# One layer with attention and routed experts on one core: normalised strips packed into two halves of 128 rows for the output projection, biases added to x by GpSimd

## The chip, the core and the metric

The kernel runs on one core of a Trainium2 chip. The core has five engines that run side by side, each with its own instruction stream: PE (TensorE, matrix products, with the weight loads PEld), DVE (VectorE), ACT (ScalarE), POOL (GpSimd) and SP (SyncE, which here only issues DMAs; ACT and POOL can issue DMAs too). They wait for one another by semaphores that the code sets by hand. The metric is the time of one execution on the device in microseconds (us); lower is better.

## What is computed

The input is x of shape 8 x 512 x 256 (8 sequences). The reference, cut:

```python
xn = layernorm(x)
kqv = xn @ W_kqv + b_kqv                      # 16 heads of 16
attn = softmax(q @ k.T / 4 + alibi(slopes), causal)
y = (attn @ v) @ W_proj + b_proj
# experts: 8, each token goes to one of them
probs = softmax(xn @ Wg); each expert takes its 512 best tokens; the rest go to their best expert
ffn = weight * gelu(xn @ W1[e]) @ W2[e]
out = x + y + ffn
```

## The kernel before

**Prologue (0 to 115 us).** Rows are normalised, turned and multiplied with W_kqv; keys and queries go to DRAM in parts (`k_parts`, `q_parts`), values stay in `vt`. At its end PE computes the part of the output that comes from the biases: the value bias goes through W_proj, since softmax weights sum to one. The result is added to row 16 of the projection weights `wp`, which has four groups g of 128 rows each, in which only rows 32j to 32j+16 are in use (head j of the group at 32j, its row of ones at 32j+16).

**The loop (115 to 529 us).** A row n of the loop is one sequence, with four groups g of four heads; G = 4n+g. A group has ten slots k; the pair (g,k) says where in a row something stands. In each slot PE computes a piece of the scores (`scores`), ACT takes the exponential of it into `pr_all` (line 735), GpSimd clears the future part of the diagonal blocks (`affine_select`, lines 605 and 608), and PE multiplies with the values one group later (`with_v`, line 1138, at slots 3 and 6). Beside that, PE and DVE already compute the row maxima of the next sequence (`max_unit`, `row_max`), from which `shift_rows` makes the shift of the exponent. ACT copies a group's product to `ysb` (`copy_y`, line 718), DVE makes the reciprocal of the sums (`invert`), and GpSimd multiplies (`normalise`, line 579). The result is a strip `yn` of 128 rows in which head j of the group stands at rows 32j to 32j+15.

**Projection.** The strips of sequence n-1 are projected in row n. PROJECT gives the slots: each tile t of 128 tokens takes four matmuls, one a group, in two pieces of two. DVE adds the result to x (`residual`, line 874, at the slots of RESIDUAL) in `xr`; SP stores the sum and loads the next x.

```python
PROJECT = {(2, 2): (0, (0, 1)), (2, 3): (0, (2, 3)), (2, 5): (1, (0, 1)), (2, 6): (1, (2, 3)),
           (2, 8): (2, (0, 1)), (2, 9): (2, (2, 3)), (3, 3): (3, (0, 1)), (3, 4): (3, (2, 3))}
RESIDUAL = {(2, 4): 0, (2, 7): 1, (3, 0): 2, (3, 5): 3}
```

**Routing.** In rows 0 to 3 DVE searches the experts' limits by bisection; in row 4 (ROUTED) it assigns tokens (`routing`), and PE counts marks in bank 7, which the projection also uses, so that the first projection of that row waits for `marks_read`. In rows 5 and 6 GpSimd scatters the tokens, four indirect DMAs a group (line 582). Also in the loop, a quarter of an expert matrix a group is loaded by SP, split by ACT and GpSimd into two f16 parts and stored. At the start of row 7 SP loads all the parts back with four DMAs of 2 MB each (lines 429, 431 and 432); they overwrite buffers of the loop (`xnp`, `vt`, `qs`).

**The tail (529 to 555 us) and the experts (555 to 675 us).** SP loads sorted rows (a DMA transpose, line 444) and token numbers (line 447), PE begins with the up products of three expert tiles, and projects the last sequence between them (`last_row`); DVE adds, SP stores the sum of x and attention, and GpSimd gathers it by token and scatters the output. The experts' loop is bound by PE.

**What sets the order.** The order on each engine is the order of its code, by slots as in the tables; SP's is the program order of its block: per group `store_quarter`, `load_quarter`, at g=3 also `shift_rows`, `store_sum`, `load_x`, and then, after a wait for the group's scores, `load_group` for two rows ahead.

## Time and profile before

| | |
|---|---|
| median of 3 runs | 688.47 us (686.81 to 691.18) |
| the profiled execution | 688.02 us, span 686.2 us |
| PE, weight loads | 561.0 us (82%), 334.7 us (49%) |
| DVE | 413.5 us (60%) |
| ACT | 331.1 us (48%) |
| POOL | 328.5 us (48%) |
| DMA queue of SP, of POOL, of ACT | 36.2%, 8.6%, 2.0% of 16 engines |
| chain that ended last | PE 40%, DVE 26%, POOL 12%, issue 10%, ACT 5%, DMA 4% |

The span is the time from the first to the last instruction in the profile; the execution's time has 1.8 us around it. A share of busy time is a mean over stages with different limits, so the stretches and the timeline of each stage are read beside it.

### The profile page before, as it was taken

What the parts mean: (1) busy time and instruction counts of PE and PEld (TensorE: products, weight loads), DVE (VectorE), ACT (ScalarE), POOL (GpSimd) and SP (SyncE); (2) the same over time, 40 slices, a digit from 0 to 9 for tenths busy, and PEclk for the clock granted to TensorE, in tenths of its full rate; (3) what the DMA queues carried; (4) which work ended last, traced back from release to release, by engine and by line L of the source; (5) the groups of instructions that cost most, each with busy time, mean ns of one, the idle gap of its engine ahead of it and who ended that gap; (6) DMA issues with size and microseconds to landing.
All of it is one profiled execution on the core that took longest, in us unless ns stands there. A gap on an engine that the chain in (4) does not pass through costs nothing.

```text
span 686.2 us, 13215 instructions
## 1 busy us (share of the span) xinstructions
PE 561.0 (82%) x4515; PEld 334.7 (49%) x4515; DVE 413.5 (60%) x819; ACT 331.1 (48%) x623; POOL 328.5 (48%) x481
## 2 busy tenths in 40 slices
PE   1878488648888989989975979998887989999992
PEld 0445254324334534535433534545333878787782
DVE  4655435959999688797798688585322333333331
ACT  3454454207665565555652456575664333333330
POOL 5647110303444354343441338787863277655552
PEclk9999799959999999999998999999999999999997
DMA  4698787591323151241421135353488445654310
GB/s 138 188 255 119 238 279 258 189 278 56 110 64 102 57 171 55 86 139 55 142 86 54 57 116 156 115 174 101 124 288 288 89 117 136 120 109 110 93 48 8
DMA packets 100671, 92.12 MB, mean 134 GB/s; under 512 B 36658, under 2 KB 89843, under 8 KB 100599
## 3 DMA queue, kind: packets, MB, share of 16 engines
q1 hardware_dynamic: 90336, 69.69, 36.2%
q0 software_dynamic: 6576, 17.91, 8.6%
q10 hardware_dynamic: 3696, 3.67, 2.0%
q8 instruction: 40, 0.66, 0.4%
q14 instruction: 23, 0.19, 0.1%
HBM read 44.22 MB, written 40.05 MB: 123 GB/s over the span
## 4 chain that ended last, share of the span: by engine, by line
PE 40%; DVE 26%; POOL 12%; issue 10%; ACT 5%; DMA 4%; SPq 2%; POOLq 0%; DVEq 0%; ACTq 0%
DVE mx L849 11%; PE ps L1248 10%; PE ps L1261 7%; PE ps L1056 7%; PE ps L1152 6%; POOL sorted_rows L582 4%; PE ps L1138 4%; POOL pr_all L605 3%; DVE mx L844 3%; PE ps L1127 2%; PE ps L1108 2%; POOL yn L579 2%; POOL w_low L572 2%; ACT pr_all L663 2%; DVE thr L907 1%
## 5 line engine op out<-in xcount | busy, mean ns | idle before, releaser
L735 ACT ACTIVATE pr_all<-ps 128x512 f32<-128x512 f32 x320 | 180.9, 598 | 178.0 <-PE ps L1127 176.7
L849 DVE TENSOR_REDUCE mx<-ps 128x2 f32<-128x768 f32 (+1 forms) x192 | 156.9, 859 | 42.0 <-PE ps L1108 41.2
L605 POOL TENSOR_SCALAR_AFFINE_SELECT pr_all<-pr_all 128x384 f32<-128x384 f32 x128 | 64.5, 529 | 177.1 <-ACT pr_all L735 177.1
L1127 PE MATMUL ps<-qs,ks 128*128 128x512 f16 (+2 forms) x448 | 116.0, 332 | 15.7 <-ACT pr_all L735 7.0
L1108 PE MATMUL ps<-ks,qs 128*128 128x384 f16 (+3 forms) x512 | 116.9, 314 | 0.0
L1105 PE MATMUL ps<-maxmask,idb 128*128 128x256 bf16 (+1 forms) x320 | 84.3, 263 | 33.1 <-DVE mx L849 19.4
L1138 PE MATMUL ps<-pr_all,vt 128*17 128x512 f32 (+3 forms) x1024 | 87.4, 461 | 4.8 <-POOL pr_all L608 4.7
L1152 PE MATMUL ps<-wp,yn 128*128 128x256 f32 x256 | 69.8, 399 | 14.3 <-DVE xr L874 8.0
L1248 PE MATMUL ps<-pr_all,xnp 128*128 128x128 f16 x936 | 77.4, 223 | 0.2
L1127 PEld LDWEIGHTS ps<-qs,ks 128*128 128x128 f16 x448 | 38.3, 100 | 74.8 <-ACT pr_all L735 41.4
L1023 DVE TENSOR_TENSOR pr_all<-pr_all 128x512 f16<-128x512 f32 x39 | 27.3, 703 | 77.4 <-ACT pr_all L749 75.1
L1248 PEld LDWEIGHTS ps<-pr_all,xnp 128*128 x936 | 64.5, 97 | 12.5 <-issue 1.3
L746 ACT ACTIVATE pr_all<-ps 128x512 f32<-128x512 f32 x39 | 23.3, 597 | 86.3 <-PE ps L1248 71.1
L1152 PEld LDWEIGHTS ps<-wp,yn 128*128 128x128 f32 x256 | 45.6, 191 | 37.7 <-issue 18.7
L1105 PEld LDWEIGHTS ps<-maxmask,idb 128*128 128x128 bf16 x320 | 32.0, 101 | 61.1 <-DVE mx L849 25.0
L1108 PEld LDWEIGHTS ps<-ks,qs 128*128 128x128 f16 x512 | 52.3, 102 | 19.2 <-issue 3.0
L1261 PE MATMUL ps<-vt,pr_all 128*128 x312 | 57.5, 273 | 4.6 <-issue 2.9
L630 POOL DMA_INDIRECT out_dram<-pr_all,token x39 | 40.0, 1026 | 33.9 <-DVE pr_all L1029 29.0
L624 POOL DMA_INDIRECT pr_all<-x_plus_attention,token x39 | 40.8, 1047 | 22.7 <-issue 21.8
L823 DVE SCALAR_TENSOR_TENSOR pr_all<-ps,bqk,pr_all 128x512 f16<-128x512 f32 x32 | 23.6, 746 | 42.4 <-ACT pr_all L688 42.3
L1138 PEld LDWEIGHTS ps<-pr_all,vt 128*17 128x17 f32 x1024 | 23.9, 98 | 45.0 <-issue 30.1
L844 DVE TENSOR_REDUCE mx<-ps 128x4 f32<-128x1024 f32 x32 | 39.0, 1219 | 10.3 <-PE ps L1108 10.1
(174 smaller groups left out, 793.7 us busy)
## 6 DMA issues: line engine op xcount, KB each, us to landing
qs<-q_parts SPq DMA_DIRECT2D x64, 100.0 KB
ks<-k_parts SPq DMA_DIRECT2D x64, 96.0 KB
sorted_rows<-ecmp POOLq DMA_DIRECT2D x1, 5160.0 KB, 22.9
k_parts<-pr_all SPq DMA_DIRECT2D x16, 256.0 KB, 3.1
q_parts<-pr_all SPq DMA_DIRECT2D x16, 256.0 KB, 2.8
xr<-in_L_attn_x_dram SPq DMA_DIRECT2D x8, 512.0 KB, 4.2
w_h<-in_L_ffn_W_dram SPq DMA_DIRECT2D x16, 256.0 KB, 3.4
w_l<-in_L_ffn_W_dram SPq DMA_DIRECT2D x16, 256.0 KB, 3.9
```

Source lines behind the costliest of these rows:

```text
L605: pool.affine_select(out=v, in_=v, compare_op=ALU.is_ge, fill=0.0, base=0, pattern=[[0, 3], [1, P]], channel_multiplier=-1).then_inc(sel_m ...
L735: act.activation(dst, src, ACT.Exp, scale=SCORE).then_inc(exp_made, 1)
L844: last = dve.tensor_reduce(mx[:, n1 % 2, :, 2 * g:2 * g + 2, 1], ps[:, 2 * (u % 2):2 * (u % 2) + 2, :].rearrange("p e (c n) -> p e c n", c=2),
L849: last = dve.tensor_reduce(mx[:, n1 % 2, :, 2 * g + c, t], ps[:, 2 * (u % 2):2 * (u % 2) + 2, c0:c0 + w], AX, ALU.max)
L1056: last = pe.matmul(out, lhs(a_, k), rhs(b_, k), start=(k == 0 and j == 0), stop=(k == EC - 1 and j == 2))
L1105: pe.matmul(diag, idb[:, :], maxmask[:, None, :].broadcast_to([P, len(ends), P]), start=True, stop=False, skip_group_check=True)
L1108: last = pe.matmul(dst[:, c0:c0 + w], qs[:, p1, e, 2 * g + i, P * t:P * (t + 1)], ks[:, p1, 2 * g + i, 0:w], start=False, stop=True, skip_ ...
L1127: last = pe.matmul(out, ks[:, p, c, t * P:(t + 1) * P], rhs, start=True, stop=True, skip_group_check=True)
L1138: last = pe.matmul(bank[6][32 * h:32 * h + VW, t * P:S], vt[:, n, t, g * HG + h, :], pr_all[:, HG * (g % 2) + h, W_AT[t]:W_AT[t] + S - t * ...
L1152: last = pe.matmul(dst, yn[:, (NG * n + g) % YN, t * P:(t + 1) * P], wp[:, g, :], start=(begin and g == 0), stop=(g == NG - 1), skip_group ...
L1248: last = pe.matmul(bank[HID_BANKS[q]][:, f * P:(f + 1) * P], w1_sb[:, bass.ds(e, 1), a_, c0:c0 + P].rearrange("p x w -> p (x w)"), xT[:, q ...
L1261: last = pe.matmul(out[:, 0:E], hh[:, q, a_, f * P:(f + 1) * P], w2p[b_][:, bass.ds(e, 1), f * E:(f + 1) * E].rearrange("p x w -> p (x w)" ...
```

## The change

It does four things.

1. The strip `yn` of each group is packed. SP copies the four used pieces of 16 rows of a strip into a half `yp` of 128 rows (`pack`, four DMAs of 16 x 512 f32, 32 KB each): groups 0 and 1 fill half 0, groups 2 and 3 half 1. There are three halves in turn. The projection of a tile takes two matmuls, not four, and they stand in one slot (PROJECT is new). PE waits for the transfers (`yp_in`), not for `y_normal`. `wp` has two parts of 128 rows and needs no zeros.
2. Biases are added to x. PE makes the sum of biases for all 128 partitions with two matmuls, DVE adds b_proj (`xb`), and GpSimd adds `xb` to `xr` once a row (`add_bias`, 128 x 1024 f32), after the row's first `normalise`; DVE's residual waits for that.
3. SP issues `pack` of two groups back at the end of each group, waiting for `y_normal`. The last two packs stand between the loads of sorted rows in the tail.
4. The four loads of expert parts are issued by ACT after its exponentials of (7, g=0), and no longer by SP.

The diff, cut to its core:

```diff
-PROJECT = {(2, 2): (0, (0, 1)), (2, 3): (0, (2, 3)), (2, 5): (1, (0, 1)), (2, 6): (1, (2, 3)),
-           (2, 8): (2, (0, 1)), (2, 9): (2, (2, 3)), (3, 3): (3, (0, 1)), (3, 4): (3, (2, 3))}
-RESIDUAL = {(2, 4): 0, (2, 7): 1, (3, 0): 2, (3, 5): 3}
+PROJECT = {(2, 4): 0, (2, 7): 1, (2, 9): 2, (3, 4): 3}
+RESIDUAL = {(2, 5): 0, (2, 8): 1, (3, 0): 2, (3, 5): 3}
...
+            def pack(G):
+                half, r0 = G // 2, HALF * (G % 2)
+                sp.wait_ge(y_normal, G + 1)
+                if half >= HALVES:
+                    sp.wait_ge(pj_made, TB * ((half - HALVES) // 2 + 1))
+                for j in range(HG):
+                    sp.dma_start(yp[r0 + D * j:r0 + D * (j + 1), half % HALVES, :], yn[32 * j:32 * j + D, G % 2, :]
+                                 ).then_inc(yp_in[G % NG], 16)
...
                     if n < B - 2:
                         sp.wait_ge(s_made, NSJ * (NG * n + g + 1))
                         load_group(n + 2, g)
+                    if NG * n + g >= 2:
+                        pack(NG * n + g - 2)
...
             for q in range(SLOTS):
+                if q == 3:
+                    pack(NG * B - 2)
+                if q == 5:
+                    pack(NG * B - 1)
                 load_rows(q, q)
...
             def normalise(G):
                 pool.wait_ge(rec_made, G + 1)
-                if G >= YN:
-                    pool.wait_ge(pj_made, TB * ((G - YN) // NG + 1))
-                pool.tensor_tensor(yn[:, G % YN, :], ysb[:, G % 2, :], rec_wide[:, :], ALU.mult).then_inc(y_normal, 1)
+                if G >= 2:
+                    pool.wait_ge(yp_in[(G - 2) % NG], 16 * HG * ((G - 2) // NG + 1))
+                pool.tensor_tensor(yn[:, G % 2, :], ysb[:, G % 2, :], rec_wide[:, :], ALU.mult).then_inc(y_normal, 1)
+
+            def add_bias(n):
+                pool.wait_ge(xr_in, 16 * (n + 1))
+                pool.tensor_tensor(xr[:, :, :], xr[:, :, :], xb[:, None, :].broadcast_to([P, TB, E]), ALU.add).then_inc(xr_made, 1)
...
             normalise(NG * B - 2)
+            add_bias(B - 1)
             normalise(NG * B - 1)
...
+            def load_experts():
+                act.wait_ge(scattered, 16 * NT)
+                for j in range(2):
+                    act.wait_ge(we_out[j], 32 * X * 2)
+                for a_ in range(2):
+                    act.dma_start(w1_sb[:, :, a_, :], ws_d[:, :, a_, 0, :].rearrange("x p w -> p x w")).then_inc(w1_in, 16)
+                act.wait_ge(s_made, NSJ * NG * (B - 1))
+                act.dma_start(w2_h, ws_d[:, :, 0, 1, :].rearrange("x p w -> p x w")).then_inc(w2_in, 16)
+                act.dma_start(w2_l, ws_d[:, :, 1, 1, :].rearrange("x p w -> p x w")).then_inc(w2_in, 16)
...
+                    if n == B - 1 and g == 0:
+                        load_experts()
...
-            def project(n, t, groups, dst, begin=True):
-                pe.wait_ge(y_normal, NG * n + groups[-1] + 1)
-                for g in groups:
-                    last = pe.matmul(dst, yn[:, (NG * n + g) % YN, t * P:(t + 1) * P], wp[:, g, :], start=(begin and g == 0),
-                                     stop=(g == NG - 1), skip_group_check=True)
+            def project(n, t, halves_, dst, begin=True):
+                for i in halves_:
+                    for g in (2 * i, 2 * i + 1):
+                        pe.wait_ge(yp_in[g], 16 * HG * (n + 1))
+                    last = pe.matmul(dst, yp[:, (2 * n + i) % HALVES, t * P:(t + 1) * P], wp[:, i, :], start=(begin and i == 0),
+                                     stop=(i == 1), skip_group_check=True)
...
-            last_row((0, 1, 2))
+            last_row(0)
             up(1, e[1])
             work_out(3)
             pe.wait_ge(y_copied, NG * B)
             up(2, e[2])
-            last_row((3,))
+            last_row(1)
```

On ACT, around the end of group 0 of row 7. `xnp`, `vt` and `qs` are the buffers that the expert parts overwrite. Before:

```order
392 L718 ACTIVATE ysb<-ps 128x512 [waits y_normal,y_made]
393 L735 ACTIVATE pr_all<-ps 128x2x256 [waits s_made]
394 L735 ACTIVATE pr_all<-ps 128x512 [waits s_made,y_made]
395 L735 ACTIVATE pr_all<-ps 128x512 [waits s_made] x3
396 L735 ACTIVATE pr_all<-ps 128x2x256 [waits s_made]
```

And in the changed kernel:

```order
392 L738 ACTIVATE ysb<-ps 128x512 [waits y_normal,y_made]
393 L755 ACTIVATE pr_all<-ps 128x2x256 [waits s_made]
394 L730 DMA xnp<-expert_parts 128x8x1024 [waits we_out1,we_out0,scattered]
395 L730 DMA xnp<-expert_parts 128x8x1024
396 L732 DMA vt<-expert_parts 128x8x1024 [waits s_made]
397 L733 DMA qs<-expert_parts 128x8x1024
398 L755 ACTIVATE pr_all<-ps 128x512 [waits s_made,y_made]
399 L755 ACTIVATE pr_all<-ps 128x512 [waits s_made] x3
```

The four loads of 2 MB have come between the last exponential of group 0 and the first of group 1.

On SP, from the last load of x to the tail. `yn<-yn` is `pack` (strip and halves share one buffer), `xr` is x, `x_plus_attention` the stored sum. Before:

```order
345 L407 DMA x_plus_attention<-xr 128x4x256 [waits xadd_made]
346 L358 DMA xr<-in_L_attn_x_dram 128x4x256 [waits xa_out]
347 L444 DMA_TRANSPOSE pr_all<-sorted_rows 128x4x128 [waits y_made]
348 L444 DMA_TRANSPOSE pr_all<-sorted_rows 128x4x128
349 L447 DMA token<-sorted_rows 128x2 x2
350 L444 DMA_TRANSPOSE pr_all<-sorted_rows 128x4x128 x2
351 L447 DMA token<-sorted_rows 128x2 x2
352 L444 DMA_TRANSPOSE pr_all<-sorted_rows 128x4x128 x2
```

And in the changed kernel:

```order
398 L353 DMA xr<-in_L_attn_x_dram 128x4x256 [waits xa_out]
399 L407 DMA yn<-yn 16x512 [waits pj_made,y_normal]
400 L407 DMA yn<-yn 16x512 x3
401 L442 DMA_TRANSPOSE pr_all<-sorted_rows 128x4x128 [waits scattered,y_made]
402 L442 DMA_TRANSPOSE pr_all<-sorted_rows 128x4x128
403 L445 DMA token<-sorted_rows 128x2 x2
404 L442 DMA_TRANSPOSE pr_all<-sorted_rows 128x4x128
405 L407 DMA yn<-yn 16x512 [waits pj_made,y_normal]
406 L407 DMA yn<-yn 16x512 x3
407 L442 DMA_TRANSPOSE pr_all<-sorted_rows 128x4x128
408 L445 DMA token<-sorted_rows 128x2 x2
409 L442 DMA_TRANSPOSE pr_all<-sorted_rows 128x4x128
```

Packs stand ahead of the first transpose, ahead of the fourth, and (after these rows) ahead of the sixth.

On PE, the end of group 2 and the start of group 3 of row 1 (`wp,yn` is the projection, `qs,ks` scores, `maxmask` and `ks,qs` the maxima). Before:

```order
757 L1152 MATMUL ps<-wp,yn 128x256 [waits y_normal,xadd_made]
758 L1152 MATMUL ps<-wp,yn 128x256
759 L1105 MATMUL ps<-maxmask,idb 128x2x128 [waits max_made]
760 L1108 MATMUL ps<-ks,qs 128x256 x2
761 L1105 MATMUL ps<-maxmask,idb 128x2x128
762 L1108 MATMUL ps<-ks,qs 128x256 x2
763 L1127 MATMUL ps<-qs,ks 128x512 [waits exp_made]
764 L1152 MATMUL ps<-wp,yn 128x256 [waits y_normal,xadd_made]
765 L1152 MATMUL ps<-wp,yn 128x256
```

And in the changed kernel:

```order
752 L1128 MATMUL ps<-maxmask,idb 128x2x128 [waits max_made]
753 L1131 MATMUL ps<-ks,qs 128x256 x2
754 L1128 MATMUL ps<-maxmask,idb 128x2x128
755 L1131 MATMUL ps<-ks,qs 128x256 x2
756 L1150 MATMUL ps<-qs,ks 128x512 [waits exp_made]
757 L1176 MATMUL ps<-wp,yn 128x256 [waits yp_in1,yp_in0,xadd_made]
758 L1176 MATMUL ps<-wp,yn 128x256 [waits yp_in3,yp_in2]
```

The third tile's two pieces at slots (2,8) and (2,9) have become one at (2,9), and its second matmul waits for the packs of groups 2 and 3.

## Rows read from the trace of the kernel before

**Rows 1.** The stretch of one row of the loop; busy us of each engine (instructions), granted clock, DMA.

```profile
248.40:296.00 47.60, 42.81 (x328) 22.28 (x324) 38.77 (x80) 28.08 (x53) 20.44 (x33) 0.96 0.35 102
```

**Rows 2.** Timeline, row n=2, group 2: start us, us, engine, line, operation, [idle before].

```profile
265.05 0.37 SPq L345 DMA_DIRECT2D qs<-q_parts  x1
...
266.69 1.27 POOL L579 TENSOR_TENSOR yn<-ysb,rec_wide 128x512 f32<-128x512 f32 x1
...
268.88 1.13 PE L1152 MATMUL ps<-wp,yn 128*128 128x256 f32 x4
...
277.42 1.13 PE L1152 MATMUL ps<-wp,yn 128*128 128x256 f32 x4 [1.27 <-DVE xr L874]
...
279.26 1.03 PE L1152 MATMUL ps<-wp,yn 128*128 128x256 f32 x4
```

**Rows 3.** Stretches of 1 us in row n=2.

```profile
254.00:255.00 1.00, 0.00 (x0) 0.00 (x0) 1.00 (x5) 0.29 (x1) 1.00 (x2) 1.00 0.61 191
...
256.00:257.00 1.00, 1.00 (x11) 0.55 (x13) 1.00 (x2) 0.03 (x1) 0.00 (x0) 0.74 0.61 204
...
259.00:260.00 1.00, 1.00 (x6) 0.62 (x5) 0.85 (x3) 0.60 (x1) 0.00 (x0) 0.55 0.00 0
```

**Rows 4.** Timeline, row n=4, group 2.

```profile
373.02 2.05 PE L1152 MATMUL ps<-wp,yn 128*128 128x256 f32 x4 [5.29 <-issue]
...
387.22 1.03 PE L1152 MATMUL ps<-wp,yn 128*128 128x256 f32 x4
```

**Rows 5.** The chain of waits, rows n=5 and 6: start us, us, what.

```profile
433.02 3.71 issue
```

**Rows 6.** Groups by form: count | busy us, mean ns | idle before.

```profile
L1152 PE MATMUL ps<-wp,yn 128*128 128x256 f32 x256 | 69.8, 399 | 14.3 <-DVE xr L874 8.0 <-issue 5.3 <-POOL yn L579 0.6
...
L579 POOL TENSOR_TENSOR yn<-ysb,rec_wide 128x512 f32<-128x512 f32 x32 | 40.7, 1273 | 3.7 <-DVE rec_wide L868 3.7
...
L498 POOL TENSOR_TENSOR xnp<-pr_all,xnp 128x1024 f16<-128x1024 f32 x8 | 17.1, 2132 | 0.7
```

**Rows 7.** Timeline, row n=7, the end of group 0.

```profile
499.83 2.78 ACT L735 ACTIVATE pr_all<-ps 128x512 f32<-128x512 f32 x5
...
500.87 1.00 SPq L429 DMA_DIRECT2D xnp<-expert_parts  x2
...
501.91 3.59 SPq L431 DMA_DIRECT2D vt<-expert_parts  x1
...
505.54 5.21 SPq L432 DMA_DIRECT2D qs<-expert_parts  x1
```

**Rows 8.** A stretch of row n=7: granted clock, DMA share, GB/s at the end.

```profile
502.50:524.00 21.50, 18.83 (x132) 9.23 (x125) 5.24 (x10) 12.31 (x24) 8.55 (x15) 1.00 1.04 382
```

**Rows 9.** Timeline of ACT at the start.

```profile
0.82 1.09 ACTq L667 DMA_DIRECT2D pr_all<-in_L_attn_x_dram  x2
1.95 1.28 ACT L670 ACT_TABLE_LOAD   x1 [1.95 <-issue]
```

**Rows 10.** Timeline, the tail.

```profile
528.46 2.63 SPq L444 DMA_TRANSPOSE pr_all<-sorted_rows  x2
...
530.23 1.27 POOL L579 TENSOR_TENSOR yn<-ysb,rec_wide 128x512 f32<-128x512 f32 x1
...
531.13 1.05 SPq L447 DMA_DIRECT2D token<-sorted_rows  x2
...
543.46 1.95 PE L1152 MATMUL ps<-wp,yn 128*128 128x256 f32 x8
...
546.24 0.38 SPq L407 DMA_DIRECT2D x_plus_attention<-xr  x1
```

**Rows 11.** DMA issues: count, KB each, median us to landing.

```profile
xr<-in_L_attn_x_dram SPq DMA_DIRECT2D x8, 512.0 KB, 4.2
...
token<-sorted_rows SPq DMA_DIRECT2D x39, 1.0 KB, 1.9
```

**Rows 12.** The chain of waits at the end of the prologue.

```profile
112.05 1.89 PE ps L1090 x8
```

76 lines of the change are left out of this document (34 added, 42 removed).

## The prediction

> **What bounds the kernel now.** I read the stretches first, then the timeline of one sequence (a row of the loop, n), then the two places where the row pattern ends. A row of the first half of the loop takes 47.6 us with PE busy for 42.8 of them and DVE for 38.8 [rows 1]: two nearly full engines that hand work to each other in order, so that a microsecond taken from PE is worth one only where PE is the late one. The timeline of row n=2, group g=2, shows such a place [rows 2]: the projection pieces stand in PE's stream (268.88, 277.42, 279.26), and PE's idle time there is 1.27 us, for a residual add. So the projections of the second half of each row are on the path. In rows 5 and 6 GpSimd is the late engine, because it sends four scatters a group there; it waits only once a row, 3.71 us at 433.02 [rows 5]. In row 7 there are no maxima left, and ACT's exponentials and PE's products alternate. In the tail, from 528 us on, PE waits for the last strip, and the gathers wait for the stored sum.
>
> **PE work removed.** One projection matmul is two records of 0.399 us mean, overlapped: a group of four takes about 1.1 us [rows 2, 6]. A row has eight such pieces (two per tile), after the change four: 4.4 us less of PE work per row, 2.2 us of it before slot (2,4), 1.1 to 2.2 in the rest of g=2, 1.1 in g=3. The prologue's bias product goes from 8 records in 1.89 us [rows 12] to 4: **-0.9 us**, as it stands on the chain there.
>
> **The new wait in each row.** The last strip of a row is normalised at 266.69 + 1.27 = 267.96 [rows 2]. Before, PE could read it at once. Now SP must see it, issue four transfers and they must land. A copy of 50 partitions takes SP 0.37 us to issue [rows 2]; nothing in the trace copies 16 partitions of SBUF into SBUF, so I take that, four in 1.5 us, with 0.6 each (2.4), half of the 1.2 that a transpose costs [rows 10], as the upper bound. For the landing the smallest transfer gives the lower bound, 1.9 us from issue [rows 11]; the upper one is 4.2 us, for 512 KB [rows 11]. The last of the four is issued at 269.1 and lands at about 271.1. PE has lost two pieces (2.2 us) by then; the value product between them waits for GpSimd's selects, so PE reaches slot (2,4)'s projection at about 268.4 and not 267.7, does its first half (0.55 us, those strips are long there), and waits 2.1 us for the second. Before, g=2's rest ran from 270.0 (268.88 + 1.13) to 280.3 (279.26 + 1.03): 10.3 us, of it four pieces (4.2), 1.27 idle, and 4.8 of other work, 0.2 of which is now done ahead of the wait. After: 271.1 + 0.55 + 4.6 + two tiles 2.2 = 278.4, with the residual add beside other work, since maxima and scores stand between the tiles. That is -1.9 us, and one piece less in g=3 (-1.0).
>
> **The clock.** PE's granted clock is at the lower of its two levels (0.5, 1.2 GHz) from 256.3 to 259.6, after PE had idled for 2.2 us from 253.7 [rows 3]. An idle time of 2.1 us at (2,4) is about as long, so I expect the fall in somewhat more than half of the rows; 3.3 us at half clock cost 1.7 us of full-speed work, **1.0 on the mean**. Rows 1 to 3: 3 x (-1.9 - 1.0 + 1.0) = **-5.7 us** (between -9 and -3.5). Here the SP queue has a second effect: the rows that shift the exponent (`shift_rows`) now stand behind four more issues, and would land at about the moment that the next row's first scores want them; I give this nothing, and up to 0.5 us a row in the range.
>
> **Row 4.** PE idles 5.29 us before the first piece, until DVE has read the marks (372.9) [rows 4]. That wait moves from slot (2,2) to (2,4): PE does the maxima and scores of slot 3, the value product and the scores of slot 4 in it, and DVE finds its maxima ready. The packed strip lands at 373 (3.1 us after a normalise that ends at about 369.5) and is hidden by the wait for the marks. Slot (2,9)'s piece ended at 388.2 (387.22 + 1.03). By the sum above: 372.9 + 1.1 + 4.6 + 2.2, and 1.0 for the lower clock at its start, is 381.8. DVE, which is full in g=3, follows 5.4 us earlier: **-5.4 us** (-6.5 to -3).
>
> **Rows 5 and 6.** The bias add is a GpSimd operation on 128x1024 f32. The nearest rows: 2.13 us for the same size with an f16 output, and twice 1.27 = 2.5 us for two of the strip multiplies [rows 6]; I take 2.4. It stands ahead of four scatters in a stretch where GpSimd never idles, so it is paid in full up to the last normalise of the row; then PE's chain of the paragraph above starts 2.4 us later and ends 1.9 (no clock fall) or 0.2 (fall) earlier in g=2. The strip's wait is half a microsecond longer here, so the fall is likelier: row 5 about +2.1 by g=3; about 1.3 us of short GpSimd waits between the rows take some back; row 6 adds the same again. The 3.71 us wait [rows 5] absorbs what is GpSimd's own. Together **+2.6 us** (-1 to +5). In the other rows GpSimd has room and the add costs nothing.
>
> **Row 7: the expert weights on ACT's queue.** This is the largest term. SP issued four loads of 2 MB: 1.00 us for two, then 3.59 and 5.21 us for the third and fourth, from 500.87 to 510.75 [rows 7]. Each is the time for which SP was held by its instruction. The DMA engines are at a share of 1.04 and 382 GB/s from 502.5 to 524 [rows 8]: the later issues wait for room. On SP nobody stood behind them. Now they stand on ACT between the exponentials of (7,0) and (7,1). That an ACT instruction waits for a DMA issue ahead of it is seen at the start: two issues from 0.82 for 1.09 us, and the table load behind them begins at 1.95 [rows 9]. ACT would start (7,1) at 500.4; it now resumes at about 510.8, and nothing else can go on, as both score banks are full, and the value product, the selects and the strip all need the exponentials. **+10.4 us**, and about +1 for PE's clock after such an idle time. The late strip costs 0.4 to 1.8 in g=2 and g=3 gives 1.1 back: 0. Row 7: **+11.4 us** (+9 to +14).
>
> The Trainium skill's page "DMA: Bandwidth & Descriptors", section "Issuing engines are not separate DMA queues", says that the sequencer's time to initiate a DMA "is usually small relative to the DMA itself". By that rule ACT would lose some 2 us and the total would be about 686; the rows of 3.59 and 5.21 us speak against it here, beside two of 0.5.
>
> **The tail.** Here the SP queue becomes the chain [rows 10]. Before, it loaded sorted rows from 528.46. Now pack(29) stands ahead of them and waits for the normalise that ends at 531.50. Behind it: pack 1.5, two transposes 2.5, tokens 1.05, transpose 1.25, pack(30) 1.5, transpose 1.25, tokens 1.05, transpose 1.25, pack(31) 1.5: until 544.4, landed at 546.5. `last_row`'s second part then starts at 546.5 (543.46 before), after more than 3 us of PE idle time, so at the lower clock: 8 records in about 3.7 us, not 1.95. Two adds of 0.7, and the sum can be stored at 551.4 against 546.24. SP is free by then (5.9 us more of transposes and tokens: 550.3). The gathers and everything behind them follow: **+5.2 us** (+3.5 with the full clock; +8 with issues of 0.6). That `last_row` falls from 24 + 8 records to 8 + 8 gains nothing, since up(0) itself now waits for its rows.
>
> **Sum.** -0.9 - 5.7 - 5.4 + 2.6 + 11.4 + 5.2 = +7.2 us on the profiled execution's 688.0 (span 686.2 and 1.8 around it): 695.2. The median of the runs shown is 688.5, half a microsecond above that execution; I write **695**. The removed memsets and the earlier small loads at the start are off the chain: 0.
>
> **Rivals.**
> (a) ACT is not held: the loads on its queue find room at once, or the exponentials pass them. The fresh queue speaks for it, the full DMA engines against it. All else as above: 695 - 10 = 685.
> (b) The strip comes later than I think, in all rows. Four small transfers stand behind the key and query rows issued around 265 [rows 2]; if they land 4.2 instead of 1.9 us after the last issue, PE loses 2.3 us in each of rows 1, 2, 3, 5, 6 and 7 (row 4 hides it): +12 with the clock fall certain, 707. It decides from about 3 us of landing on, as the whole gain of a row is then gone. Against it: the DMA engines have spare time there.
> (c) The waits hide better than I think: no clock falls and ACT held as above: -3 in rows 1 to 3, -2 in 5 and 6, -1.7 in the tail: 688. This is the low end of my own case.
> (d) The change doesn't do what it says: the halved products don't shorten PE's stream, because a full 128-row product costs more than a sparse one. The records now already have 128 rows; I give it 2%.
>
> **How the numbers follow.** Forecast 60% (689 to 701), (a) 15%, (b) 13%, (c) and (d) with other gains of the loop 12%. The range 684 to 704 leaves out the worse part of (b) and a better loop together with (a). About 1% (682 to 695) is what the measurement tells from no change; my forecast lies at that edge, so the slower and the unchanged share of it are about equal, (a) counts mostly as unchanged, (b) as slower. Faster 0.11, same 0.43, slower 0.46.
>
> **What would show it.** Right: ACT idle for some 10 us near 500 with its own queue issuing; L1152's busy time halved to 35 us; 2 us of PE idle before the second half of (2,4)'s product in rows 1 to 3; the 5.29 us wait gone or shorter; the sum stored some 5 us later after the last exponential. Wrong: exponentials running between the weight loads, packs that take over 3 us to land, or a first half of the loop that is not shorter by 11 us by the end of row 4.

## The result, and the profile after

| | before | changed |
|---|---|---|
| median | 687.66 us (686.81 to 691.18, 4 runs) | 720.80 us (719.16 to 726.68, 4 runs) |
| profiled execution's span | 686.2 us | 718.6 us |
| PE, weight loads | 561.0, 334.7 us | 548.7, 317.6 us |
| SP's own share of the chain | 2% | 12% |

The ratio is 1.047, 95% interval 1.0438 to 1.0503: slower by 33 us, outside the predicted range of 684 to 704. Executions more than 1.5% above the fastest of their kernel are left out of the ratios and intervals, here and below, but not out of the medians. PE has 12 us less to do and the kernel is 32 us longer, so the answer is in the waits. The ends of each group's tenth exponential (ACT, line 735 before, 755 after) cut both timelines in the same places; this table is what the rest of the text goes by.

| stretch | before | changed | difference | forecast |
|---|---|---|---|---|
| start to (0,3) | 192.70 | 191.30 | -1.4 | -0.9 |
| rows 1 to 3 | 145.98 | 146.51 | +0.5 | -5.7 |
| row 4 | 60.63 | 61.07 | +0.4 | -5.4 |
| rows 5 and 6 | 91.90 | 98.88 | +7.0 | +2.6 |
| row 7: (7,0), (7,1), (7,2), (7,3) | 9.25, 7.81, 11.10, 9.48 | 12.07, 19.69, 15.47, 8.18 | +2.8, +11.9, +4.4, -1.3 | +11.4 together |
| last exponential to the store of the sum | 17.40 | 25.85 | +8.4 | +5.2 |
| from there to the end | 139.99 | 139.53 | -0.5 | 0 |

The chain by engine (part 4 of the page; SPq is SP issuing), and the projection's group of part 5, which answers to [rows 6]; behind the bar stand the busy us and the mean in ns, then the idle time ahead and what ended it:

```profile
PE 34%; DVE 19%; SPq 12%; POOL 10%; issue 10%; DMA 7%; ACT 5%; ACTq 1%; POOLq 0%; DVEq 0%
...
L1176 PE MATMUL ps<-wp,yn 128*128 128x256 f32 x128 | 40.7, 442 | 26.3 <-DMA yn<-yn 22.6
```

The projection's busy time fell from 69.8 to 40.7 us, not to 35, and 22.6 us of waiting for packed strips came with it. A record takes no longer when all 128 rows are in use: the median is 379 ns in both kernels, and four records take 1.03 us in both (at 279.26 before, at 279.00 after). The mean rose from 399 to 442 ns because 27 of 128 records took over 500 ns, most of them in stretches with a granted clock of 0.50 behind a wait; before, 4 of 256 did. The view of waits of PE names a second newcomer (us in total, times, longest); before, the second one stood there once, at the start of the loop, with 5.4 us:

```profile
PE ps L1176 <- DMA yn<-yn: 22.6, 7, 3.9
...
PE ps L1150 <- DMA qs<-cc: 19.1, 7, 5.2
PE ps L1150 <- ACT pr_all L755: 16.3, 13, 10.8
```

`qs<-cc` is `shift_rows`, which the prediction gave "nothing". The timelines of GpSimd, SP and PE in row n=2, from the last strip of the row before to the start of row 3, show both waits (they answer to [rows 2]):

```profile
266.18 1.28 POOL L578 TENSOR_TENSOR yn<-ysb,rec_wide 128x512 f32<-128x512 f32 x1
...
267.49 2.42 SPq L407 DMA_DIRECT2D yn<-yn  x4
...
271.41 0.67 PE L1176 MATMUL ps<-wp,yn 128*128 128x256 f32 x2 [3.18 <-DMA yn<-yn]
...
279.00 1.03 PE L1176 MATMUL ps<-wp,yn 128*128 128x256 f32 x4
...
280.33 0.36 SPq L340 DMA_DIRECT2D qs<-q_parts  x1
282.60 2.41 SPq L407 DMA_DIRECT2D yn<-yn  x4
285.05 0.58 SPq L390 DMA_DIRECT2D expert_parts<-w_h  x1
...
286.65 2.43 SPq L397 DMA_DIRECT2D qs<-cc  x4
...
290.60 0.38 PE L1150 MATMUL ps<-qs,ks 128*128 128x512 f16 x1 [1.71 <-DMA qs<-cc]
```

The chain of waits gives the same place piece by piece: four issues of 0.5 to 0.6 us, and then the landing.

```profile
268.68 0.59 SPq L407
...
269.31 1.97 DMA yn<-yn
```

A pack takes SP 2.42 us, not 1.5; its landing takes 1.97 us, as assumed (1.9). PE waits 3.18 us, and group 2's last piece ends at 280.03, where 278.4 was forecast and 280.29 measured before. Then the next pack and the quarters stand ahead of the shift rows, and row 3's first scores wait again. That pack costs more than its issues: SP issues nothing from 280.69 to 282.60, because it waits there until GpSimd has normalised the strip (until 282.57). DVE has the data of the shift rows (`cc`) ready at 282.6, and they are issued at 286.65: 2.4 us of pack and 1.6 us of quarters come first, which SP could have issued while it stood. SP stands so for 1.8 to 1.9 us in each of rows 1 to 3. The kernel before already held the price of such a transfer, in a row that the prediction did not look at. Its SP timeline, four copies of 8 KB within SBUF:

```profile
235.25 2.42 SPq L402 DMA_DIRECT2D qs<-cc  x4
```

PE's clock after the 3.18 us of idle time (stretches of 1 us, the clock is the third number from the end; compare [rows 3]):

```profile
271.00:272.00 1.00, 0.59 (x3) 0.48 (x4) 0.00 (x0) 0.00 (x0) 0.00 (x0) 1.00 0.79 260
...
273.00:274.00 1.00, 1.00 (x9) 0.23 (x12) 1.00 (x3) 1.00 (x2) 0.00 (x0) 0.50 0.45 159
```

In row 7 ACT is held by its four loads, as forecast (it answers to [rows 7]); PE stands still behind it and comes back at the lower clock (0.50 from 514 to 524):

```profile
509.17 0.38 ACTq L730 DMA_DIRECT2D xnp<-expert_parts  x1
...
510.22 3.90 ACTq L732 DMA_DIRECT2D vt<-expert_parts  x1
514.15 6.14 ACTq L733 DMA_DIRECT2D qs<-expert_parts  x1
520.39 1.09 ACT L755 ACTIVATE pr_all<-ps 128x512 f32<-128x512 f32 x2 [10.55 <-issue]
```

Stretches of 5 us, the clock again third from the end:

```profile
514.00:519.00 5.00, 0.00 (x0) 0.00 (x0) 0.00 (x0) 0.00 (x0) 0.79 (x1) 0.50 1.06 366
519.00:524.00 5.00, 2.95 (x13) 0.51 (x14) 0.00 (x0) 2.17 (x4) 0.00 (x0) 0.50 1.05 361
```

The strip that is projected in (7,2) is then packed from 532.22 on. PE waits 3.81 us for it, and its landing is the last piece of that wait in the chain:

```profile
534.03 2.46 DMA yn<-yn
```

And the tail, which answers to [rows 10]: packs ahead of the transposes, and PE's wait for the last strip ends at 574.0.

```profile
555.87 2.87 SPq L407 DMA_DIRECT2D yn<-yn  x4
558.84 2.63 SPq L442 DMA_TRANSPOSE pr_all<-sorted_rows  x2
...
570.10 2.42 SPq L407 DMA_DIRECT2D yn<-yn  x4
...
579.03 0.43 SPq L412 DMA_DIRECT2D x_plus_attention<-xr  x1
```

### The profile page after: what moved, and what is told of

It reads as the page before. It is cut to its first block, busy times and chain, and to the rows that moved or that the text cites. A ratio compares the mean times of both kernels' runs of the same rounds, so it can differ in the third digit from the quotient of the medians.

```text
span 718.6 us, 13126 instructions
## 1 busy us (share of the span) xinstructions
PE 548.7 (76%) x4383; PEld 317.6 (44%) x4383; DVE 414.8 (58%) x819; ACT 331.5 (46%) x623; POOL 344.8 (48%) x487
## 4 chain that ended last, share of the span: by engine, by line
PE 34%; DVE 19%; SPq 12%; POOL 10%; issue 10%; DMA 7%; ACT 5%; ACTq 1%; POOLq 0%; DVEq 0%
PE ps L1272 9%; DVE mx L871 8%; PE ps L1285 7%; PE ps L1078 5%; SPq L407 4%; PE ps L1161 3%; PE ps L1150 3%; PE ps L1131 3%; POOL pr_all L608 3%; POOL yn L578 2%; DMA qs<-cc 2%; DVE mx L866 2%; POOL w_low L572 2%; DMA yn<-yn 2%; SPq L316 2%
## 5 line engine op out<-in xcount | busy, mean ns | idle before, releaser
L1150 PE MATMUL ps<-qs,ks 128*128 128x512 f16 (+2 forms) x448 | 120.7, 344 | 38.2 <-DMA qs<-cc 19.1
L608 POOL TENSOR_SCALAR_AFFINE_SELECT pr_all<-pr_all 128x384 f32<-128x384 f32 x128 | 63.9, 523 | 161.6 <-ACT pr_all L755 161.4
L1131 PE MATMUL ps<-ks,qs 128*128 128x384 f16 (+3 forms) x512 | 118.7, 318 | 0.0
L1161 PE MATMUL ps<-pr_all,vt 128*17 128x512 f32 (+3 forms) x1024 | 93.7, 489 | 9.9 <-POOL pr_all L611 9.9
L1272 PE MATMUL ps<-pr_all,xnp 128*128 128x128 f16 x936 | 78.9, 225 | 4.8 <-DMA pr_all<-sorted_rows 4.8
L1176 PE MATMUL ps<-wp,yn 128*128 128x256 f32 x128 | 40.7, 442 | 26.3 <-DMA yn<-yn 22.6
L572 POOL TENSOR_TENSOR w_low<-w_h 128x512 f16<-128x512 f32 x16 | 18.5, 1156 | 63.1 <-ACT w_h L722 63.1
L1285 PE MATMUL ps<-qs,pr_all 128*128 x156 | 43.1, 276 | 0.0
```

What stands on the lines that cost most here:

```text
L608: pool.affine_select(out=v, in_=v, compare_op=ALU.is_ge, fill=0.0, base=0, pattern=[[0, 3], [1, P]], channel_multiplier=-1).then_inc(sel_m ...
L1131: last = pe.matmul(dst[:, c0:c0 + w], qs[:, p1, e, 2 * g + i, P * t:P * (t + 1)], ks[:, p1, 2 * g + i, 0:w], start=False, stop=True, skip_ ...
L1150: last = pe.matmul(out, ks[:, p, c, t * P:(t + 1) * P], rhs, start=True, stop=True, skip_group_check=True)
L1161: last = pe.matmul(bank[6][32 * h:32 * h + VW, t * P:S], vt[:, n, t, g * HG + h, :], pr_all[:, HG * (g % 2) + h, W_AT[t]:W_AT[t] + S - t * ...
L1176: last = pe.matmul(dst, yp[:, (2 * n + i) % HALVES, t * P:(t + 1) * P], wp[:, i, :], start=(begin and i == 0), stop=(i == 1), skip_group_c ...
L1272: last = pe.matmul(bank[HID_BANKS[q]][:, f * P:(f + 1) * P], w1_sb[:, bass.ds(e, 1), a_, c0:c0 + P].rearrange("p x w -> p (x w)"), xT[:, q ...
```

## The experiments

shift_first, project_late, loads_sp and no_bias ran on one chip, on which the kernel before takes 689.2 us. All others ran on four slower chips, on which the kernel before itself takes 717.8 to 723.1 us: most of that is the experts' part, from the first gather to the end (153 to 165 us there, 135 to 137 on the first chip), and a few us in rows 5 to 7. So each ratio is to the kernel before on the same chip, and mechanisms are read from stretches. On one of the slower chips the changed kernel's own ratio is 1.0352 and not 1.047 (last experiment); ratios from the slower chips are held against that one, with the reserve that it was measured on one of the four. The expected times in us were written for the first chip. How far a stretch scatters between executions is seen where the code does not differ: the changed kernel's stream up to the end of (7,0) was profiled in six kernels; rows 1 to 3 took 145.6 to 149.5 us, row 4 57.9 to 61.1, and rows 5, 6 and (7,0) 107.6 to 115.0. The stream of the kernel before, profiled twice up to there, took 146.0 and 146.3, 60.6 and 61.9, 101.1 and 106.8 (the second of each on a slower chip).

**The shift rows ahead of the pack.** In SP's loop `shift_rows(n + 1)` moves from group 3 to the end of group 2:

```diff
+                    if g == 2 and n < B - 1:
+                        shift_rows(n + 1)
                     if NG * n + g >= 2:
                         pack(NG * n + g - 2)
```

> The changed kernel with one edit: SP issues shift_rows of the next row at the end of group 2, ahead of that group's pack, not in group 3 behind the pack and the quarters. Theory (the four pack issues of 0.6 us, and the quarters behind them, make shift_rows land late, and PE's first scores of the next row wait for it: 13.9 us in six waits between rows, with the clock falling after the longer ones): shift_rows starts 2.4 to 3.9 us earlier, PE's waits for qs<-cc in rows 1 to 6 disappear, and the kernel takes 14 to 20 us less than the changed one, 701 to 707 us. Rival (the wait only uncovers another one behind it, DVE's maxima or the next strip, since PE and DVE are both nearly full): the waits for qs<-cc go, but the time falls by less than 5 us, to 716 or more.

Measured: 712.85 us, ratio 1.0349 (1.0303 to 1.0395), some 8 us less. All waits for `qs<-cc` but the first are gone; rows 1 to 3 take 142.1 us (4.4 less), and the first groups of rows 2 and 3 are back at the 9.2 us of the kernel before (12.8 and 10.2 in the changed kernel). Row 4 takes 57.6, 3.4 less than in the changed kernel's first profile, but its scatter reaches down to 57.9. The time lies between the two expectations: for 13.9 us of waits the median fell by 8. The strip waits stay (23.1 us). The edit takes the shift rows out from behind both the pack's issues and SP's wait for the strip; it does not tell the two apart.

**The projections later.**

```diff
-PROJECT = {(2, 4): 0, (2, 7): 1, (2, 9): 2, (3, 4): 3}
+PROJECT = {(2, 6): 0, (2, 8): 1, (3, 3): 2, (3, 5): 3}
```

RESIDUAL follows one slot behind each, and one wait of PE ahead of `turn_max` asks for one residual add less.

> The changed kernel with the four projections at slots (2,6), (2,8), (3,3), (3,5), their residual adds one slot behind, so that the last strip of a row has 2 to 4 us more to be packed. Theory (PE's seven waits for yn<-yn, 22.6 us with 3.2 to 3.9 us each, and the fall of PE's clock behind them, are paid in full in rows 1 to 3 and 5 to 7): the waits go, and the kernel takes 10 to 16 us less, 705 to 711 us. Rival (in rows 5 and 6 GpSimd is the late engine, and DVE's maxima set the pace in g=2 of the other rows, so that PE's wait only moves to another releaser): 0 to 5 us less.

Measured: 714.62 us, ratio 1.0368 (1.0313 to 1.0423), some 7 us less. The waits for strips fall from 22.6 to 7.6 us, and 12.4 us of waits for DVE's residual adds appear. Rows 1 to 3 take 141.9 us (4.6 less), but row 4, where DVE routes, 64.1 (3.0 more), and (7,2) takes 10.3, not 15.5, though ACT's loads stand where they stood. This time too lies between the two expectations.

**Both.**

> The changed kernel with both edits of the loop: shift_rows ahead of the pack, and the projections at slots (2,6), (2,8), (3,3), (3,5). Alone they took 8.0 and 6.2 us off the time (1.0349 and 1.0368 against 1.047 of the changed kernel, as ratios to the kernel before). Theory (two different waits at two places of the row): they add up, 14 to 17 us less, 704 to 707 us. Rival (both only give slack to the same late engine, DVE or GpSimd): 8 to 11 us less, 710 to 713 us.

Measured on a slower chip: ratio 1.0230 (1.0171 to 1.0289). Against 1.047 that would be the theory's 16 us, but against the 1.0352 of a slower chip it is 9. On the same chip tail_act, whose code is the changed kernel's up to the last exponential, ends that one 7.5 us later. Rows 1 to 3 take 141.2 us, hardly less than with either alone (142.1 and 141.9). So in those rows the theory falls: the gains don't add up. That another engine then sets the pace is likely; which one was not looked into. With both, rows 1 to 3 are 4.8 us below the kernel before: most of the 5.7 us that the forecast saw was there to be had.

**The issue cost itself.** Each pack in eight transfers of 8 rows, not four of 16, the bytes unchanged.

```diff
-                    sp.dma_start(yp[r0 + D * j:r0 + D * (j + 1), ...], yn[32 * j:32 * j + D, ...]
+                    for d in (0, D // 2):
+                        sp.dma_start(yp[r0 + D * j + d:r0 + D * j + d + D // 2, ...], ...
```

> The changed kernel with each pack in eight transfers of 8 rows, not four of 16: twice the issues, the same bytes. Theory (SP's issue time per transfer, 0.6 us whatever its size, is what makes strips, shift rows and the tail late): a pack takes SP 4.8 us; each of rows 1 to 3, 5 and 6 loses 2.4 us more at the strip wait and up to 2.4 us more at the wait for shift rows, row 7 2.4 us, the tail 7 us for its three packs; plus 20 to 35 us on the changed kernel, a ratio of 1.075 to 1.10. Rival (an issue costs by its rows, so that eight small ones take no longer than four, or the landing sets the wait): under 8 us more, a ratio under 1.06.

Measured: 792.08 us, ratio 1.1068 (1.0959 to 1.1177). SP's timeline and PE's, row 2:

```profile
276.51 5.33 SPq L408 DMA_DIRECT2D yn<-yn  x8
```

```profile
283.32 1.19 PE L1177 MATMUL ps<-wp,yn 128*128 128x256 f32 x2 [6.08 <-DMA yn<-yn]
```

An issue costs SP no less for half the rows (0.67 us each). PE's wait grows by the 2.9 us that the pack grew, and the time from the last issue to PE's start stays at 1.5 us; rows 1 to 3 take 165.3 us, 6.3 a row more, and the store of the sum comes 35.8 us after the last exponential. That the count of issues on SP sets the wait for a strip is thereby shown. The ratio lies above my range, though its interval reaches into it. In rows 1 to 3 the waits for shift rows grew as well, to 4.5 and 4.9 us ahead of rows 2 to 4 (1.7 to 3.1 in the changed kernel).

**The loads of 8 MB, in other places.** First back on SP, where they were:

> The changed kernel with one edit: the four 2 MB loads of expert parts are issued by SP again, at their old place (after the quarters of row 7, group 0, ahead of pack). Theory (ACT is held by its own DMA issues for 10.6 us and PE behind it loses 11.9 us in group (7,1)): ACT's 10.55 us wait goes, and the kernel takes 10 to 12 us less, 709 to 711 us. Rival (the two packs of (6,2) and (6,3) now stand behind the loads on SP, and the projection at slot (2,4) of row 7 waits for them, 4 to 5 us more than now): only 5 to 7 us less, 714 to 716 us, with a wait for yn<-yn of 8 us in row 7.

Measured: 724.00 us, ratio 1.0506 (1.0458 to 1.0555), no gain at all. SP's timeline, and PE's:

```profile
515.73 6.63 SPq L422 DMA_DIRECT2D qs<-expert_parts  x1
522.47 9.67 SPq L407 DMA_DIRECT2D yn<-yn  x8
```

```profile
539.21 1.19 PE L1175 MATMUL ps<-wp,yn 128*128 128x256 f32 x2 [16.57 <-DMA yn<-yn]
```

(7,1) is 7.8 us again, ACT's wait is gone, and (7,2) takes 27.7. The packs are issued behind the loads, and land behind them too: PE can go on at 539, 7 us after the last issue of the second. The rival was right in kind and too small (16.6 us of waiting, not 8). Loads and packs can't stand on one queue in this order.

The same part of the change alone, in the kernel before (its loads issued by ACT):

> The kernel before with one part of the change alone: the four 2 MB loads issued by ACT after its exponentials of row 7, group 0. Theory: ACT is held for 10 to 11 us behind its own issues and nothing hides it, plus 10 to 12 us, a ratio of 1.014 to 1.018. Rival (ACT was held in the changed kernel because packs and loads share room, and here it isn't): a ratio under 1.006.

Measured: 734.57 us, ratio 1.0202 (1.0151 to 1.0253). (7,1) takes 18.7 us, not 7.8: 10.9 more. (7,2) and (7,3) are as before, and (7,0), ahead of the loads, takes the 10.6 us that it also takes in before_bias on the same chip. That is the forecast's largest term, in pure form. The ratio is worth 14 to 15 us and lies above the range of the theory, with an interval that reaches into it; where the further 3 us would lie, the one profile doesn't show.

One group later on SP, behind the pack of (6,3):

> The changed kernel with the four 2 MB loads issued by SP, but one group later than where SP issued them before: behind the pack of (6,3) at the end of row 7, group 1. Theory (what cost 12 us with the loads on ACT was ACT being held; what cost 12 us with the loads at SP's old place was that the two packs behind them were issued late and landed only when the 8 MB ahead of them on the same queue had moved, 16.6 us of PE waiting): with both packs ahead of the loads neither happens. Group (7,1) ends 11 to 12 us earlier, group (7,2) takes as long as in the changed kernel, and the time is 707 to 711 us. Rival (the packs of row 7 that are now behind the loads and the weights' later arrival hold up the tail): the gain of (7,1) is given back from (7,3) on, 715 us or more.

Measured: ratio 1.0298 (1.0236 to 1.0360), where the changed kernel has 1.0352 on another slower chip; the intervals overlap. (7,1) takes 9.0 us, 10 less than with the loads on ACT, and (7,2) 14.8, but the sum is stored 32.7 us after the last exponential, 6 to 7 later than in the changed kernel: most of the gain is given back in the tail, as the rival has it.

On GpSimd's queue, behind its work of (7,0):

> The changed kernel with the four 2 MB loads issued by GpSimd, behind its selects and its normalise of row 7, group 0. Theory (the place where ACT lost 10.6 us and SP's packs lost 12 us is a hardware queue that has no room for 8 MB at once; GpSimd's own queue is another kind, on which one store of 5 MB held it for 2.2 us): GpSimd is held for 4 to 9 us in a group in which it is half idle, ACT and the packs are free, group (7,1) ends 11 to 12 us earlier relative to (7,0) and the time is 1.5% to 1.8% lower than the changed kernel's, a ratio of 1.029 to 1.032 to the kernel before. Rival (GpSimd is held as long as ACT was, and its selects of (7,1) stand behind): less than 4 us, a ratio of 1.041 or more.

Measured: 732.6, 732.8, 743.7 and 750.6 us, against a median of 720.9 for the kernel before. The first two give a ratio of 1.017, all four by their median 1.024; runs that far apart give no interval, so only the stretches are read. GpSimd's timeline, and PE's:

```profile
511.90 1.90 POOL L590 DMA_DIRECT2D xnp<-expert_parts  x2
513.78 0.90 POOL L592 DMA_DIRECT2D vt<-expert_parts  x1
514.66 0.90 POOL L593 DMA_DIRECT2D qs<-expert_parts  x1
```

```profile
527.48 1.19 PE L1176 MATMUL ps<-wp,yn 128*128 128x256 f32 x2 [5.92 <-DMA yn<-yn]
```

Four loads hold GpSimd for 3.7 us, where ACT was held for 11.1, and (7,1) takes 9.0 us, as the theory has it. But (7,2) takes 19.0: the pack, issued by SP and not behind the loads, is held up all the same. The chain of waits has its landing at 6.07 us, where row 2 of the changed kernel had 1.97:

```profile
521.27 6.07 DMA yn<-yn
```

Each of these two places together with the edits of the loop and of the tail (below), all_four with the loads late on SP, five with them on GpSimd:

> Both edits of the loop, the 2 MB loads on SP behind the pack of (6,3), the last three packs on ACT, and in the tail the last strip normalised ahead of the last bias add. If all the losses are told apart rightly and add up (14 to 17, 10 to 12, 6 to 9 us), the time is 683 to 690 us, level with the kernel before. Rival (the gains overlap in row 7 and the tail, and GpSimd's bias adds of 2.4 us in rows 5 and 6 and the later strips still cost their 7 us): 692 to 698 us.

> All edits that helped, together: shift_rows ahead of the pack, projections at (2,6), (2,8), (3,3), (3,5), the 2 MB loads on GpSimd, the last three packs on ACT, and the last strip normalised ahead of the last bias add. Theory (the five losses lie at different places): the last exponential ends within 2 us of the kernel before's 528.8, the sum is stored 18 to 19 us behind it, and the ratio is 0.996 to 1.004. Rival (a sixth loss is left, the 2.4 us of bias adds in front of GpSimd's scatters): 1.006 to 1.012.

Measured: 1.0109 (1.0063 to 1.0154) and 1.0046 (1.0010 to 1.0081). all_four is at its last exponential at 527.8 us, 1 us below the profile of the kernel before (which is of a faster chip), and then stores the sum 30.8 us later, not 17.4; five loses its time in (7,2) (16.0 us) and stores the sum after 19.3. The ratio of all_four is the rival's; that of five lies between theory and rival, and its interval reaches both. Then with the loads held back until the strip of (6,3) had landed:

> As five, but GpSimd issues the four 2 MB loads only in group 2 of row 7, after the strip of (6,3) has landed in its half. Theory (in row 7 the pack's 32 KB transfers land late because the DMA engines work off 8 MB of loads that were issued ahead of them, though on another queue): the strip wait of row 7 falls from 8 us to under 2, (7,1) to (7,2) takes about 11 us, and the ratio is 0.995 to 1.001, 4 to 5 us under five. Rival (the experts' weights now come late for the first up product, or the wait has another cause): no less than five, 1.003 or more.

Measured: 1.0140 (1.0059 to 1.0221). (7,2) is down to 9.8 us and PE's strip wait to 0.6. The strip lands 1.95 us after its last issue, where five has 5.96; the place of the loads is all that differs:

```profile
520.66 1.95 DMA yn<-yn
```

So it is shown that loads under way hold up the strip, though another engine issued them. The rival decides the time, since GpSimd's next strip and the last load of x now wait instead, and the store comes 30.0 us after the last exponential. GpSimd's timeline:

```profile
549.28 1.26 POOL L574 TENSOR_TENSOR yn<-ysb,rec_wide 128x512 f32<-128x512 f32 x1 [8.58 <-DMA yn<-yn]
```

**The tail.** The last three packs are issued by ACT after its last copy; SP's loop stops before them.

```diff
-                if q == 3:
-                    pack(NG * B - 2)
-                if q == 5:
-                    pack(NG * B - 1)
+            for G in range(NG * B - 3, NG * B):   # on ACT, behind copy_y
+                pack(G)
```

> The changed kernel with the last three packs (groups 1 to 3 of row 7) issued by ACT, after its last copy, and no longer by SP between the loads of sorted rows. Theory (in the tail SP's queue is the chain: twelve issues of 0.6 us stand between the transposes, so up(0) waits 4.8 us for its rows and last_row 3.9 us for its strips, and the sum is stored 25.9 us after the last exponential instead of 17.4): the sum is stored about 18 us after it and the kernel takes 6 to 9 us less, 712 to 715 us. Rival (ACT's first gelu stands behind the packs and the experts start late, or PE is ready to go on without the stored sum): less than 3 us.

Measured: ratio 1.0229 (1.0150 to 1.0308). The sum is stored 18.8 us after the last exponential, 7.0 less than in the changed kernel, as the theory says. Against 1.0352 the ratio is worth 9 us, which is the upper end of the expected 6 to 9, with intervals that overlap.

**The bias.** Left out in the changed kernel, and a pass over x of the same size added to the kernel before:

> The changed kernel without the addition of the biases to x (add_bias only passes its semaphore on, so the output lacks the bias terms). Theory: add_bias costs 2.4 us of GpSimd in each of rows 5 and 6, where GpSimd never idles, and 1.5 us in row 4, where DVE's product of the routing takes 1.88 us beside it instead of 0.42; with what follows in the tail the kernel takes 5 to 8 us less, 713 to 716 us. Rival (GpSimd has room for it, the rows wait for strips and shift rows): less than 2 us.

> The kernel before with GpSimd's pass over x alone, at the places of add_bias: a product with ones of 128x1024 elements, which leaves x as it is and costs GpSimd what the bias add costs, with DVE's residual adds waiting for it. Theory (GpSimd is the late engine in rows 5 and 6, and DVE's products run slower beside GpSimd's): 2.4 us in each of rows 5 and 6 and 1 to 2 us in row 4, plus 5 to 8 us, a ratio of 1.007 to 1.012. Rival (short waits of GpSimd take it in): a ratio under 1.004.

Measured: 717.52 us, ratio 1.0427 (1.0362 to 1.0492), and 1.0081 (1.0043 to 1.0118). The first interval overlaps that of the changed kernel, so the time alone doesn't show the 3 us. Without it rows 5, 6 and (7,0) take 105.6 us, below all six executions with it (107.6 to 115.0). In the kernel before they take 108.8 with the pass and 106.8 without on the same chip, and row 4 0.6 more. The pair of profiles gives 2.5 us and the ratio 5.8 (3 to 8.5 by its interval), so the size is known only roughly. Row 4 has a part of its own in the changed kernel (DVE's timeline, beside GpSimd's add at 353.25 to 355.77; the same product takes 0.42 us before):

```profile
354.17 1.88 DVE L936 TENSOR_TENSOR rr<-rr,r 128x256 f32<-128x256 f32 x1
```

The pair of runs shows that GpSimd's pass over x is the reason: without it (no_bias) the product takes 0.43 us, with it in the kernel before (before_bias) 1.66. In both cases with the pass the product ends 0.3 us behind it.

**Bias of rows 5 and 6 on DVE,** first with the loads as in six, then as in five, then with half of the loads held back:

```diff
+                        if n in (5, 6) and (g, k) == (1, 5):
+                            dve.wait_ge(xr_in, 16 * n)
+                            dve.tensor_tensor(xr[:, :, :], xr[:, :, :], xb[:, None, :]..., ALU.add)
```

The residual adds of these two rows wait for this add.

> As six, but the bias adds of rows 5 and 6 are made by DVE, in group 1, and no longer by GpSimd ahead of its scatters. Theory (GpSimd never idles in those rows, so its 2.4 us a row are paid in full): rows 5 and 6 together are 4 to 5 us shorter than in six, a ratio of 0.988 to 0.996. Rival (other short waits take the place, or DVE is no less late there): within 1.5 us of six.

> As five (loads on GpSimd right behind group (7,0)), with the bias adds of rows 5 and 6 on DVE as in seven. Theory: the 5 us that the bias adds cost come off five's 1.0046, a ratio of 0.995 to 1.001; the strip wait of 5 to 8 us in (7,2) stays. Rival (the edits overlap): 1.002 to 1.006.

> As eight, but only the first 4 MB (the parts of W1) are loaded behind group (7,0); the other 4 MB are issued in group 2 of row 7, after the strip of (6,3) has landed. Theory (a small transfer is late by what of the 8 MB is still ahead of it in the DMA engines, so 4 MB at a time hold up less): (7,1) to (7,2) takes 11 to 13 us instead of 16, the sum is stored 19 to 23 us behind the last exponential, and the ratio is 0.990 to 0.998. Rival (the delay only moves to the last row's strips and to the loads of sorted rows, as in six): the store is 25 us or more behind the last exponential and the ratio is no better than eight's.

Measured: seven 1.0113 (1.0067 to 1.0159), eight 0.9929 (0.9900 to 0.9958), split 0.9953 (0.9923 to 0.9983). Seven and six ran on one chip: rows 5, 6 and (7,0) take 102.3 us against 107.9, the 5 us of the theory, but the ratio is only 0.3% lower and the intervals overlap. In eight they take 106.3 and in split, the same code up to there, 102.9; five had 106.4. So that the move helps is likely, and its size is not measured. Seven lies above the theory's range, eight below it; eight and split are below the kernel before, by 0.7% and 0.5%, with intervals that leave out 1. In split (7,2) takes 14.8 us (15.9 in eight) and not 11 to 13, and the sum is stored after 19.6 (19.5): holding half of the loads back is worth nothing that these intervals tell.

**The changed kernel again,** beside eight and split on a slower chip:

> The changed kernel as it is, beside the two others of this call. If the chip alone made the earlier ratios lower (stages behind the loop are longer there for both kernels and hide part of the tail's loss), its ratio is 1.035 to 1.045; if the chip doesn't matter it is 1.047 within its interval, some 34 us over the kernel before.

Measured: 749.35 us against 723.13, ratio 1.0352 (1.0296 to 1.0408). The loss is smaller there, 26 us. Two parts of the difference can be seen. Rows 5, 6 and (7,0) take 106.8 us in the stream of the kernel before on a slower chip and 110.8 to 115.0 in that of the changed kernel, so 4 to 8 us more, where it was 9.9. And from the store of the sum to the end loads_pool takes 161.4 us where the two variants of the kernel before on its chip take 163.9 and 164.2, so some 2 us of the tail's loss may be hidden behind it, as the expectation has it. The rest is not settled. Eight is 31 us below the changed kernel on the same chip.

## Why the prediction was wrong

**The steps that failed.** The forecast was +7.2 us and the profiles give +32.4. Of the 25 us between them rows 1 to 4 have 12.0, row 7 6.4, rows 5 and 6 4.4 and the tail 3.2. Two steps failed, and one term beside them.

"A copy of 50 partitions takes SP 0.37 us to issue; nothing in the trace copies 16 partitions of SBUF into SBUF, so I take that." The trace did hold the nearer row, `shift_rows`' own copies within SBUF, four in 2.42 us. With its 0.6 the pack is 2.4 us, my upper bound, and that is what it measured. It was priced at 1.5 us from a transfer that came from DRAM.

"The rows that shift the exponent (`shift_rows`) now stand behind four more issues ... I give this nothing." The mechanism was written down and then left without a price (0.5 us a row in the range). SP is done with them 2.9 us later than before in row 1 (240.52, not 237.67) and 3.8 in row 2, and PE, which has less to do, wants them earlier: 1.2 to 3.5 us of waiting at the start of each row from 1 to 7 but one, 13.9 in all. The step also saw issues alone; SP stands 1.8 to 1.9 us for the strip itself ahead of the pack, which in row 2 pushed 1.6 us of other issues in front of the shift rows. shift_first takes back 4.4 us in rows 1 to 3, of the 6.2 by which they missed the forecast.

The term is the strip in row 7, put at 0.4 to 1.8 us in group 2: it cost 4.4 us in (7,2).

**Term by term.** Rows 1 to 3: +0.5, not -5.7; with both waits removed, -4.8. By groups, the first groups of the three rows took 4.8 us more in all, the shift rows' part, and group 1 0.2 less a row. Group 2 took 0.15 us less a row and not 0.9 (1.9 less 1.0 for the clock), which is about what the longer issues cost. Group 3 took 1.06 less a row, for which 1.0 was forecast.

Row 4: +0.4, not -5.4. The sum in the text gives 6.4 us (388.2 less 381.8) and takes 5.4 without saying why. PE's timeline has the marks' wait at its new place, (2,4):

```profile
376.05 2.04 PE L1176 MATMUL ps<-wp,yn 128*128 128x256 f32 x4 [3.54 <-issue]
```

From the marks to the end of the third tile PE takes 10.5 us and not 15.4, 4.9 less where the sum had 6.4, and (4,2) is 4.4 us shorter; so that part came nearly as foreseen. But DVE has read the marks at 375.9 and not at 372.9: (4,0) gained 2.1 us by the shift rows (4,1) 1.5 and (4,3) 1.3. DVE's product at 1.88 us lies in (4,1), but in before_bias it takes 1.66 and (4,1) is as before, so no run explains these two.

By the end of row 4 the loop was to be 11 us shorter, the text's own sign of being wrong; it is 0.4 us shorter, the start included.

Rows 5 and 6: +7.0, not +2.6. Group 2 takes 4.9 and 4.4 us more than before, with strip waits of 2.5 and 2.7 us, and the bias has 2.5 us by the stretches and 5.8 by the ratio of before_bias. The scatter of the stream (107.6 to 115.0 us with (7,0)) is larger than the miss, so no closer account is shown.

Row 7: ACT's hold was right (10.55 us, 10.9 alone in the kernel before, for 10.4), and with the clock behind it (7,1) is 11.9 longer. The strip's 4.4 us in (7,2) are a wait like that of the other rows: 3.81 us, with issues of 2.4 and a landing of 2.46, and a granted clock of 0.50 behind it. The 8 MB have nearly all moved by then (the DMA share falls from 1.03 to 0.34 between 532 and 535), and the landing is only 0.5 us longer than in row 2; in project_late, with the same loads on ACT, (7,2) takes 10.3. (7,0) took 2.8 more, with 3.5 us of waiting for shift rows at its start. (7,3) took 1.3 less, as foreseen (1.1).

The tail: +8.4, for which the text had "+8 with issues of 0.6". Prologue: -1.4, but the start of the first exponential scatters from 150.1 to 154.5 between executions of nearly one code, so neither number says anything.

**The rivals.** (a) fell: nothing passed the loads. (b), a strip that comes later, was right in its direction and not in its cause: the landing was as assumed, the issue longer; and its 707 us were still 14 short. (c) fell. (d) fell too: a full product takes as long as a sparse one (median 379 ns in both), and PE's projection costs 40.7 us and not 35 because more of it runs at the lower clock.

The Trainium skill says on its page "DMA: Bandwidth & Descriptors", in "Issuing engines are not separate DMA queues", that DMAs of all engines run on the same 16 DMA engines, and that the time to initiate one "is usually small relative to the DMA itself". The first half agrees with loads_pool and six (a landing of 6.07 us with another engine's loads under way, 1.95 without them). Against the second stand 2.42 us of issues for a landing of 1.97, and the 11.1 us for which four loads hold ACT.

The Trainium skill's page "SBUF — State Buffer", section "Who interferes with whom", says that a DVE instruction with two SBUF inputs contends with a GpSimd instruction that reads SBUF. The trace agrees: DVE's product of two SBUF tiles takes 1.88 us beside GpSimd's add and ends 0.3 us behind it, and 0.43 without the add. That GpSimd's pass is the reason is shown by no_bias and before_bias; that it is the ports, no run here tells.

## What to carry to other kernels

Price a new transfer by the nearest kind (source, target, partitions) in the trace, per issue and not per byte, and then walk down the issuing queue: each instruction behind it comes later by the sum of issues, and by what the queue waits for ahead of them; what waits for that is a term of its own. A bulk load cost something in every place tried beside the packs: on ACT and SP it held the issuing engine for some 10 us, on GpSimd for 3.7, and while it ran a small transfer of another engine landed 4 us later. It belongs where no small transfer is waited for. What a change loses by placement need not be lost with it: with its issues, its projections and the bias adds of two rows placed elsewhere (eight), it is 0.7% ahead of the kernel before. Whether those placements would also help the kernel before was not tried, so that the packing itself gains anything is not shown.
